# Reading two of six scatter tables while the last pairs of experts still run

## What is computed

```python
x = layernorm(x + attention(x))
router = sigmoid(x @ gate_w)          # 64 experts in 8 groups, 4 groups kept, the 6 best experts of a token
for each expert e:                    # at most 48 tokens each
    rows   = tokens that chose e, in order
    hidden = silu(rows @ w_gate[e]) * (rows @ w_up[e])
    y[tokens] += weight * (hidden @ w_down[e])
shared = silu(x @ ws_gate) * (x @ ws_up) @ ws_down
out = layernorm(x + y + shared)
```

## Time and profile before

| | us |
|---|---|
| median of three runs | 1110.91 (1107.33 to 1110.97) |
| the profiled execution, its own time | 1108.96 |
| its span, first to last instruction | 1107.1 |
| TensorE, VectorE, ScalarE, POOL busy | 999.0, 645.5, 520.7, 367.6 |
| mean granted TensorE clock | 0.965 |

### The profile page before, as it was taken

One profiled execution on the slowest core, in us unless ns is written; L12 is line 12 of the kernel. 1 busy time (PEld: TensorE's weight loads), 2 busy tenths in 40 slices (PEclk: granted clock), 3 DMA queues, 4 the chain that ended last, 5 costly groups with the idle time before them and its releaser, 6 DMA issues.

```text
span 1107.1 us, 17285 instructions
## 1 busy us (share of the span) xinstructions
PE 999.0 (90%) x5448; PEld 752.2 (68%) x5448; DVE 645.5 (58%) x1666; ACT 520.7 (47%) x1151; POOL 367.6 (33%) x406
## 2 busy tenths in 40 slices
PE   6999998589999999999998899999999998639835
PEld 4888887466678787777676667777777776526412
DVE  5777666365575666565655765565756647324326
ACT  4333334445564656464644554554655645126402
POOL 5766666113322212103143323313131120126821
PEclk9999999899999999999998999999999999859968
DMA  7455333533332211111214323432211123988687
GB/s 232 159 186 186 115 130 135 175 93 114 86 96 70 59 58 58 60 44 32 86 55 111 110 83 91 138 92 84 72 40 58 34 62 105 244 235 207 89 256 295
DMA packets 108952, 128.34 MB, mean 116 GB/s; under 512 B 16465, under 2 KB 75973, under 8 KB 108864
## 3 DMA queue, kind: packets, MB, share of 16 engines
q1 hardware_dynamic: 86752, 98.92, 28.6%
q10 hardware_dynamic: 13408, 22.09, 6.6%
q0 software_dynamic: 8704, 6.24, 3.6%
HBM read 81.99 MB, written 58.59 MB: 127 GB/s over the span
## 4 chain that ended last, share of the span: by engine, by line
PE 76%; DVE 7%; issue 5%; DMA 4%; ACT 3%; SPq 3%; POOL 1%; ACTq 0%; DVEq 0%; POOLq 0%
PE s_ps L1019 16%; PE o_ps L1046 12%; PE ring L1029 11%; PE ring L1058 9%; PE o_ps L1049 6%; PE s_ps L990 6%; PE ring L990 5%; SPq L693 2%; PE s_ps L1112 2%; DVE neg_max L1218 2%; PE s_ps L997 1%; PE s_ps L1022 1%; ACT probs L873 1%; PE ring L1073 1%; DMA sums<-erow,goal_u 1%
## 5 line engine op out<-in xcount | busy, mean ns | idle before, releaser
L1218 DVE TENSOR_REDUCE neg_max<-s_ps 128x1 f32<-128x128 f32 (+7 forms) x256 | 191.4, 751 | 133.8 <-PE s_ps L1022 122.2
L873 ACT ACTIVATE probs<-s_ps,neg_max 128x128 f32<-128x128 f32 (+7 forms) x256 | 189.3, 740 | 135.5 <-DVE neg_max L1218 125.1
L1019 PE MATMUL s_ps<-kt,qt_hi 128*128 128x512 f32 (+3 forms) x768 | 241.0, 395 | 4.8 <-POOL qt_lo L754 2.5
L754 POOL TENSOR_TENSOR qt_lo<-q_raw,qt_hi 128x512 fp32r<-128x512 f32 x64 | 81.8, 1279 | 411.4 <-ACT qt_hi L799 411.4
L1029 PE MATMUL ring<-ident,probs 128*128 128x128 f32 x1152 | 175.8, 275 | 17.6 <-ACT probs L873 14.9
L1019 PEld LDWEIGHTS s_ps<-kt,qt_hi 128*128 128x128 f32 x768 | 137.7, 192 | 60.0 <-issue 35.0
L1046 PE MATMUL o_ps<-pt,v 128*128 128x512 f32 x336 | 174.2, 601 | 1.7 <-DVE ot L1237 1.5
L1029 PEld LDWEIGHTS ring<-ident,probs 128*128 128x128 f32 x1152 | 128.3, 141 | 48.6 <-issue 37.4
L882 ACT ACTIVATE pt<-ring 128x512 f32<-128x512 f32 x168 | 99.3, 593 | 82.6 <-PE ring L1029 72.8
L799 ACT ACTIVATE pt_hi<-ring 128x512 fp32r<-128x512 f32 x120 | 70.8, 594 | 133.3 <-PE ring L1029 132.6
L1019 PE MATMUL s_ps<-kt,qt_lo 128*128 128x512 f32 (+3 forms) x384 | 133.0, 346 | 0.0
(11 more groups left out here) (196 smaller groups left out, 1524.9 us busy)
## 6 DMA issues: line engine op xcount, KB each, us to landing
q_rows<-q_out SPq DMA_DIRECT2D x64, 256.0 KB, 2.0
q_raw<-q_rows ACTq DMA_DIRECT2D x64, 256.0 KB, 2.6
inv_row<-inverses SPq DMA_DIRECT2D x64, 256.0 KB
fsum<-sums SPq DMA_DIRECT2D x48, 256.0 KB, 8.2
sums<-blank SPq DMA_DIRECT2D x16, 640.0 KB
wexp<-in_L_ffn_w_gate_dram SPq DMA_DIRECT2D x32, 192.0 KB, 5.7
wexp<-in_L_ffn_w_up_dram SPq DMA_DIRECT2D x32, 192.0 KB, 6.1
wexp<-in_L_ffn_w_down_dram SPq DMA_DIRECT2D x32, 192.0 KB, 7.1
```

The lines of the kernel that those rows point to most:

```text
L754: pool.tensor_tensor(qt_lo[:, u % 2, :], q_raw[:, u % QB, :], qt_hi[:, u % 2, :].bitcast(F32), ALU.subtract).then_inc(q_ready, 1)
L873: act.activation(probs[:, u % 2, h, 0:blocks(u) * P], s_ps[:, n % 2, score_cols(n)], ACT.Exp, bias=neg_max[:, n % 8:n % 8 + 1], accum_out= ...
L1019: pe.matmul(s_ps[:, n % 2, c + a:c + e], q[qp], k[kp][:, a:e], start=(qp == kp == 0), stop=(qp == 1 and not last))
L1218: dve.tensor_reduce(neg_max[:, n % 8:n % 8 + 1], s_ps[:, n % 2, score_cols(n)], AX_X, ALU.max, negate=True).then_inc(max_ready, 1)
```

## The change

From pair 15 (`THREE`) on the pairs take turns over two pairs of tables instead of three; `TURN_OF[n]` is the turn of pair n and `TURN_AT[n]` how many earlier pairs had it. Tables 4 and 5 (`LATE` = 4 and up) are then complete once scatter 14 has landed. SP loads them, slice by slice, into a tile of their own, `fsum_early`: two loads behind the landing of scatters 16, 17, 19, 20, 22, 23, 25 and 26. At the end 32 loads remain. TensorE adds the two early tables first and then waits for the slice's other four; VectorE adds the two early parts of an odd slice to each other before it waits, then table 0 and that sum, and then tables 1 to 3. The number of additions is the same. The tiles of the end are laid out so that `fsum_early` does not lie over the homes 0 to 3, which the pairs 28 to 31 use again.

```diff
+LATE = TABLES - 2
+THREE = 15
+TURN_OF = [n % 3 if n < THREE else (n - THREE) % 2 for n in range(PAIRS)]
+TURN_AT = [TURN_OF[:n].count(TURN_OF[n]) for n in range(PAIRS)]
...
-        fsum = sb("fsum", [P, FINAL, TABLES, PER_ROW * M], F32, fin)
+        fout = sb("fout", [P, FINAL, PER_ROW * M], F32, fin)
+        homes_again = sb("homes_again", [P, 1024], F32, fin)
+        fsum_early = sb("fsum_early", [P, FINAL, TABLES - LATE, PER_ROW * M], F32, fin)
+        fsum = sb("fsum", [P, FINAL, LATE, PER_ROW * M], F32, fin)
...
+            sp.wait_ge(erow_sent[TURNS - 1], 16 * TURN_OF.count(TURNS - 1))
+            for c in range(FINAL):
+                n = THREE + 1 + 3 * c // 2
+                sp.wait_ge(erow_sent[TURN_OF[n]], 16 * (TURN_AT[n] + 1))
+                for a in range(LATE, TABLES):
+                    sp.dma_start(fsum_early[:, c, a - LATE, :], token_rows[a][:, c, :]
+                                 ).then_inc(fsum_early_loaded, 16)
             for n in range(TURNS):
-                sp.wait_ge(erow_sent[n], 16 * len(range(n, PAIRS, TURNS)))
+                sp.wait_ge(erow_sent[n], 16 * TURN_OF.count(n))
             for c in range(FINAL):
-                for a in range(TABLES):
+                for a in range(LATE):
                     sp.dma_start(fsum[:, c, a, :], token_rows[a][:, c, :]).then_inc(fsum_loaded[c], 16)
...
-                used(pool, erow_sent[n % TURNS], 16 * (n // TURNS))
+                used(pool, erow_sent[TURN_OF[n]], 16 * TURN_AT[n])
...
-                ).then_inc(erow_sent[n % TURNS], 16)
+                ).then_inc(erow_sent[TURN_OF[n]], 16)
...
-                used(act, erow_sent[(n - EB) % TURNS], 16 * ((n - EB) // TURNS + 1))
+                if n >= EB:
+                    act.wait_ge(erow_sent[TURN_OF[n - EB]], 16 * (TURN_AT[n - EB] + 1))
...
-                pe.wait_ge(fsum_loaded[c], 16 * TABLES)
-                for a in range(TABLES):
-                    ins = pe.matmul(sum_rows(c), ident[:, :], fsum[:, c, a, :], start=(a == 0), stop=(a == TABLES - 1))
+                pe.wait_ge(fsum_early_loaded, 16 * FINAL * (TABLES - LATE))
+                for a in range(TABLES - LATE):
+                    pe.matmul(sum_rows(c), ident[:, :], fsum_early[:, c, a, :], start=(a == 0), stop=False)
+                pe.wait_ge(fsum_loaded[c], 16 * LATE)
+                for a in range(LATE):
+                    ins = pe.matmul(sum_rows(c), ident[:, :], fsum[:, c, a, :], start=False, stop=(a == LATE - 1))
...
-                dve.wait_ge(fsum_loaded[c], 16 * TABLES)
-                for a in range(1, TABLES):
+                dve.wait_ge(fsum_early_loaded, 16 * FINAL * (TABLES - LATE))
+                add(dve.tensor_tensor(fsum_early[:, c, 0, :], fsum_early[:, c, 0, :], fsum_early[:, c, 1, :], ALU.add))
+                dve.wait_ge(fsum_loaded[c], 16 * LATE)
+                add(dve.tensor_tensor(fsum[:, c, 0, :], fsum[:, c, 0, :], fsum_early[:, c, 0, :], ALU.add))
+                for a in range(1, LATE):
                     add(dve.tensor_tensor(fsum[:, c, 0, :], fsum[:, c, 0, :], fsum[:, c, a, :], ALU.add))
```

More of the change, by code:

```diff
@@ L261, in build @@
         slots_left = sb("slots_left", [P, E], F32)
-        row_base = sb("row_base", [P, -(-PAIRS // TURNS) * TURNS], F32)
+        row_base = sb("row_base", [P, PAIRS + 1], F32)
         spare = sb("spare", [P, 1], F32)
@@ L373, in build @@
         nmr = sb("nmr", [P, FINAL, PER_ROW], F32, fin)
-        fout = sb("fout", [P, FINAL, PER_ROW * M], F32, fin)
         fin.close()
@@ L443, in build @@
         scattered = [sem(f"scattered{n}") for n in range(2)]
-        stood = sem("stood")
         dve_own = sem("dve_own")
@@ L458, in build @@
         fsum_added = sem("fsum_added")
+        fsum_early_loaded = sem("fsum_early_loaded")
         fsum_loaded = [sem(f"fsum_loaded{n}") for n in range(FINAL)]
@@ L734, in _ @@
             for e in range(2):
-                link(pool.iota(row_base[e * HALF:(e + 1) * HALF, :], pattern=[[0, -(-PAIRS // TURNS)], [2 * TABLE, TURNS]],
+                half = slice(e * HALF, (e + 1) * HALF)
+                link(pool.iota(row_base[half, 0:THREE], pattern=[[0, THREE // TURNS], [2 * TABLE, TURNS]],
+                               base=e * TABLE, channel_multiplier=0, allow_small_or_imprecise_dtypes=True))
+                link(pool.iota(row_base[half, THREE:], pattern=[[0, (PAIRS + 1 - THREE) // 2], [2 * TABLE, 2]],
                                base=e * TABLE, channel_multiplier=0, allow_small_or_imprecise_dtypes=True))
```

## The result

| | before | the change |
|---|---|---|
| median of nine runs each, us | 1111.28 | 1118.46 (1117.04 to 1120.94) |
| ratio, 95% interval | | 1.0065 (1.0053 to 1.0077) |
| profiled execution: own time, span | 1108.96, 1107.1 | 1117.96, 1115.4 |
| scatter 15 to scatter 31 (starts) | 29.06 | 43.16 |
| first final load to the end of VectorE's last round | 42.33 | 32.47 |

The change is 0.65% slower. The two stages of the prediction moved in opposite directions: +14.1 us in the scatters and -9.9 us in the final reading. What is left of the difference between the two profiles lies ahead of both: the first scatter starts at 995.15 before and at 999.68 after.

The account below looks back on a forecast made before the run. At the program's end, POOL's issue pace bounds the scatters, then load transfers bound the final reading. 7.1 + 3.8 - 9.7 = +1.2 us on 1108.96 gives 1110.2, a median of 1112, range 1106 to 1119.

Parts of the forecast that it names:

- the queue rival: Scatters 16 to 28 each take 5.01 us beside early loads, steps 2.88: +5.2 us, 1116 median; chance 0.17 beyond 0.5% slower.
- Two turns, +7.1: Scatters from 17 on wait for the landing of n-2, so odd ones step by 4.35 us: +7.1 us.
- The loads beside the scatters, +3.8: Eight groups of two early loads delay scatters; +3.8 us taken between 2.7 and 6.9.
- The row of the pair's weights: Three 192 KB weight loads made scatters 15 and 16 land in 5.01 and 4.14 us instead of 3.61; scaled, 6.9 us.
- two chains of scatters alternate: Early-load groups fall on both alternating scatter chains, so a delay was counted half.
- The final reading, -9.7: 32 final loads instead of 48, VectorE becoming the limit: 32.65 us after first issue instead of 42.33, -9.7 us.
- POOL's steps of "2.2 to 2.7": Sign in the new trace: scatters from pair 17 on start on POOL at steps of 2.2 to 2.7 us.
- scatters beside loads pass 5.1 us on average: Sign that the forecast is wrong: slower by over 0.5% from a mean of about 5.1 us per scatter on.
- The step of (landing + 0.74)/2: With two turns POOL's wait allows one scatter each 4.35/2 = 2.18 us, from a 3.61 us landing plus 0.74.
- Two turns suffice: Rival: scatters land in 2.78 us, so two turns lose nothing; about 1101 us; chance 0.06 with other gains beyond 0.5%.
- The loads fit into the gaps: Rival: early loads beside the scatters cost only 0 to 1.5 us; about 1109 us median; chance 0.15.
- the change does what it says: Rival denying this: SP reaches early loads late, they run beside final ones, 7.1 us stays without gain; 1118; chance 0.02.

Follow-up runs that it names:

- the second profile before: The kernel before, unaltered, profiled again: scatter 15 to 31 took 29.05 us, first final load to end 42.79 us.
- two turns alone: Kernel before with the change's turns only, all 48 loads after all scatters: scatter 15 to 31 38.47 and 37.33 us, ratio 1.0095.
- POOL's help: The change, but POOL instead of VectorE adds the two early tables of each odd slice: rounds 5.35 us instead of 6.06, ratio 1.0039.
- three turns with half the loads: The change with three turns throughout and one early load of input x per group instead of two: scatter 15 to 31 took 29.60 us.

## Why the prediction was right or wrong

The range, 1106 to 1119, held the 1118.46, but only by half a microsecond, and it reached so far only because it took in a part of the queue rival. The outcome I held likely did not come: the time rose by 7.2 us, and I had given 0.75 to less than 5.6 either way and 0.19 to more. The stages, the waits and their directions were right; two of the three terms were too small, and both errors point the same way. By its terms:

- **Two turns, +7.1.** Right in its mechanism, too small. Measured alone: +8.3 and +9.4. The steady step (4.35 us for two scatters) came as worked out. Missing were single delays: the late start of scatter 19, 1.1 us in every profile, which the earlier trace rows and POOL's timeline before already held, and a slow landing. With three turns most of such a delay goes into the slack (a landing of 4.61 us in the second profile before cost POOL 0.17 us), with two each is paid (4.63 us, 1.1 us). I had priced the chain at its mean landing and left no room for either.
- **The loads beside the scatters, +3.8.** This step failed. Against two turns alone (mean 37.9) the change's two profiles are 5.3 and 7.8 us longer, about 6.5. What was too small is the time that a group adds to the landings: I let half of its 1.36 us hit a scatter, 0.68, and had no row for that. The landings of scatters 15 to 29 grew by 11 and 14 us over those with two turns alone, 1.4 and 1.7 us a group, the whole transfer or more. The row of the pair's weights, 1.93 us for its three loads (6.9 in all, scaled to the size of these), was the better guide. The other halving, that a delay counts half, came out in size (5.3 of 11, 7.8 of 14 us), but not for its reason, "two chains of scatters alternate": POOL issues in order, so the scatters go in couples, and a couple waits for the slower chain; what stretches both landings of a couple is paid once. In the timeline after, scatter 21 follows 20 after 1.76 us, having waited for 20's turn and not for its own.
- **The final reading, -9.7.** Right: -9.9 in the first profile, and on the mean of two each -9.8. VectorE took over as the bound as predicted, shown by its rows and by POOL's help. Its parts came too: the first addition 9.0 us after the first issue (8.9), the first round 5.2 (5.3), the other three 18.3 (18.45). TensorE did delay the first round in one experiment by about 1 us, which I had counted at nothing.
- **The rest.** POOL's steps of "2.2 to 2.7" are 2.70 on the mean in the first profile (43.16/16) and 2.86 in the second. The last start, expected between 1064 and 1071, came at 1074.98, 4.2 of it from the later start of scatter 15. The sign "scatters beside loads pass 5.1 us on average" did not show: over scatters 16 to 28, as that rival counts, the means are 4.54 and 4.68 us, and still the time passed 0.5%. The step of (landing + 0.74)/2 behind that sign takes both landings of a couple at their mean, where POOL pays the slower of the two, and leaves out scatter 19's 1.1 us.

Of the rivals, "the queue behind the loads" came nearest: its estimate was +5.2 us, by 5.01 us per scatter and steps of 2.88; the steps were nearly that long, the landings not. "Two turns suffice" is excluded by the experiment with two turns alone. "The loads fit into the gaps" describes three turns with half the loads (+0.55) and nothing else that was tried. That the change does what it says is shown by SP's row at 1038.29 and by the scatters that wait two turns back.

The sum of the profiles gives +4 and +7 (scatter 15 to the end 79.08 and 82.40 against 75.05 and 75.54), the runs +7.2 and +6.1. The 3 us between the first profile and its runs are not explained; the spread of the attention part and of the landings is as large. What decides how far a group of loads stretches a landing, beyond the time of its transfer, stays open: the trace says that it does, not in which order the DMA engines serve the two queues.

## What to carry to other kernels

A wait for a DMA's landing is free as long as enough other DMAs are in turn; count the slack (turns x issue interval - landing - restart, here 3 x 1.76 - 3.6 - 0.83 = 0.85 us) before giving a turn away, and remember that slack also swallows most of a rare slow landing. Transfers moved under such a loop cost nothing while a landing stays inside the slack (+0.55 us for eight loads here) and half to two thirds of what they save once it doesn't (+4.5 with three turns, about +6.5 with two, for sixteen that save 9.8). And a row that prices the very thing, however unlike it looks, is better than a share of a transfer time for which there is no row. Such rows can also show a wait that is longer at one place than at all others, as at scatter 19: hold each restart against the landing that released it.

## What was not expected of the hardware

- POOL comes back from a landing later than ScalarE does: where both wait for the same scatter, ScalarE starts first and POOL's DMA instruction 0.74 to 0.77 us after it, in every profile (scatters 10 and 19 excepted).
- Two scatters start later than that. In all 14 profiles scatter 19 starts 1.93 us after the landing that it waits for, whatever that landing took and whether it is that of 16 or of 17, and in most of them scatter 10 does so too (1.94 us); a scatter that waits starts 0.83 us after it otherwise, but for a few single ones. What sets these two apart is open: the profile names no cause that differs from their neighbours', and their code is the same.
- A small load of instructions may hold up a scatter by about a microsecond. With two turns alone, scatter 21 starts at 1045.53 and lets ScalarE go at 1050.24, 4.71 us. The DMA view of 1045.5 to 1050.5 has one instruction load in it, which runs on one of the 16 engines:

```profile
q0 software_dynamic: 342, 0.30, 50.9%
q8 instruction: 1, 0.02, 1.2%
```

  In the second profile the load came earlier and scatter 19 was the slow one. Before, a load of the same kind at 1040.55 lies beside scatters 20 to 22, which land in 3.5 to 3.7 us as always. So it is a coincidence in time, seen in several profiles and missing in others, and no experiment was made on it.
